# Latents and keys and values of both token halves made in tile pairs, in an attention stage between two expert layers

## The chip, the cores and the metric

One Trainium2 chip, one of its cores. The metric is device time in microseconds of one execution, the median of the timed runs. Engines are called as the profile calls them: PE (TensorE's matmuls), PEld (its weight loads), DVE (VectorE), ACT (ScalarE), POOL (GpSimd), SP (SyncE, which here only issues DMAs).

## What is computed

A macaron block: half of a mixture of experts on the layer-normalized tokens, attention, half of the same mixture again, each added to its input. 16 batches of 1024 tokens, 256 wide; 8 experts, the best 2 of each token. The attention, which the change touches:

```python
q = x @ W_q                                   # x: normalized, 16 x 1024 x 256
latent_kv = (x @ W_k + x @ W_v) @ W_down_kv   # 64 wide
k_rec = latent_kv @ W_up_k                    # 16 heads of 16
v_rec = latent_kv @ W_up_v
scores = (q k_rec^T) / sqrt(256) * exp(-0.01 |t - t'|)
out = softmax(scores) v_rec
return out @ W_o
```

All matmuls touched by the change are in fp32, which PE runs as two passes each.

## The kernel before

Three stages follow each other: the first mixture, the attention (class `Attention`), the second mixture. The attention runs all engines over one list, `self.plan`, that `order()` writes out in advance. Every engine walks through the whole list and executes its own part of each item, with waits on semaphores between engines; so the list sets the order on each engine's queue, POOL's and SP's too.

**The loop of the plan.** Heads go in pairs, 8 pairs a batch, 128 pairs in all. `order()` loops over `s`; one pass is called a slot here. Its main item is `("step", score, turn)`: four score pieces (L1163; q times k for 512 keys each, into the ring of four banks 0 to 3, read by DVE's row maxima at L1453 or, once in eight slots, by a multiply at L1448) and four turned pieces (L1172 and L1176; scores transposed, into the ring of three banks 5 to 7, read by ACT's exponential at L1376). The score pieces run 12 slots ahead of the turned ones. At the end of a slot stands `("W", p, kb)` (L1312): four matmuls of 17 columns in four column tiles, that weigh the values. Between step and W a slot takes what is due: every eighth slot the maxima of a pair (`max`, L1457 and L1462) and, in that slot and the next, a `sub` on POOL each (L1691), then norm, output projection (`out`, L1288), routing of the tokens for the next stage (`r_...` items, with POOL's centers at L1672, and its scatters, four indirect DMAs at L1684), and one portion each of two generators: `gather_order(b + 1)` (tokens of the next batch: gathers, two indirect DMAs each at L1613, adds at L1620 and L1622, centers, transposes "turn") and `unit_order(b)`. `None` in a generator ends its portion, so it says how many slots the generator takes.

**`unit_order(b)`**, for b of 1 to 15: two slots of latents (one chunk of 512 tokens each), 8 projections of six slots each, four slots of values. Projections 0 to 3 are queries (two halves of the heads times two chunks), 4 to 7 keys. A projection is made by PE in a bank of the score ring (L1220 queries, L1223 keys), read by DVE twice with the decay factors (L1551, into buffer `qs[:, i % 2]`), and split into three bf16 parts: `cast` 0 (ACT, L1349), `rest` 0 (POOL, L1651), two slots on `cast` 1, one slot later `rest` 1, one slot later the next projection. `send` writes the parts to HBM, `stack` fetches them in the layout of a head pair. At L1551's item DVE waits for `part_lo` of projection i - 2, that is for its second `rest`, since that is when its `qs` buffer is free. The gathers of the next batch begin in the slot after projection 3. Batch 0 has no steps beside it and another order; its rests are made by DVE.

**Latents, keys, values.** A latent (L1208) takes a turn bank, and PE multiplies 128 rows by 64 columns, twice 128 rows deep; ACT copies 64 x 512 to `lat` (L1343). A key projection is one matmul 64 rows deep, over the chunk's 512 columns of `lat`. A values unit is two matmuls 64 rows deep (L1230), and ACT copies it to `V` (L1354).

Of the kernel before, what the change touches and what calls it, by code (L numbers as in the profile page):

```python
# [700 lines left out]
class Attention:  # L701
# [4 lines left out]
    def __init__(self, nc, sig, x0, ys, tables, x1, x2, parts, mdram, xs, routes, cst, w, begin):  # L706
# [12 lines left out]
        self.XR, self.xT, self.lat = sb("XR", [128, 8, D]), sb("xT", [128, 2, S]), sb("lat", [DL, S])  # L719
# [9 lines left out]
        self.wd, self.wuk, self.wuv = sb("wd", [128, 2, DL]), sb("wuk", [DL, D]), sb("wuv", [DL, D])  # L729
# [27 lines left out]
        self.loaded, self.x_in = sig.new("a_loaded", 16 * 15), sig.new("a_x_in", 48 * B)  # L757
# [139 lines left out]
    def unit_order(self, b):  # L897
        for ch in range(2):
            yield from (("latent", b, ch), None)
        if not b:  # L900
            for i in range(0, 8, 2):
# [4 lines left out]
                if i == 2:  # L906
                    yield from (("values", 0, t2) for t2 in range(4))
            return
        for i in range(8):
            yield from (("project", b, i), None, ("cast", b, i, 0), None, ("rest", b, i, 0))  # L910
            if i:
                yield ("send", b, i - 1)
            yield from (None, None, ("cast", b, i, 1), None, ("rest", b, i, 1), None)
        for t2 in range(4):
            yield ("values", b, t2)
            if t2 == 2:
# [141 lines left out]
    def sync(self, e, w):  # L1058
# [8 lines left out]
        for dst, src in ((self.ident[:], cst["ident"]), (self.decay[:, 0], cst["decn"]), (self.decay[:, 1], cst["decp"]),  # L1067
                         (self.Dm[:], cst["dm"]), (self.wq[:], fold(wt["q"])), (self.wk[:], fold(wt["k"])),
                         (self.wv, fold(wt["v"])), (self.wd[:], fold(wt["down"])), (self.wuk[:], wt["upk"]),
                         (self.wuv[:], wt["upv"]), (self.wo[:], fold(wt["o"])),  # L1070
# [79 lines left out]
    def tensor(self, e, w, ps, bank):  # L1150
# [3 lines left out]
        w.wait_ge(*self.loaded.at(240))  # L1154
# [24 lines left out]
        for item in self.plan:  # L1179
# [23 lines left out]
            if kind == "latent":  # L1203
                b, ch = at
                w.wait_ge(*self.result("weight", 2))
                w.wait_ge(*self.result("turn", b, ch, 1))
                for k in range(2):
                    ins = e.matmul(to[0:DL, 0:512], self.wkv[:, k, :], self.xT[:, k, 512 * ch:512 * ch + 512], start=(k == 0), stop=(k == 1))  # L1208
                ins.then_inc(self.filled.sem, 1)
            if kind == "project":  # L1210
# [3 lines left out]
                w.wait_ge(*self.s_read.at(z - 3))  # L1214
                of = bank[z % 4]
                z += 1
                if not keys:
                    w.wait_ge(*self.result("turn", b, ch, 1))
                    for k in range(2):
                        ins = e.matmul(of, self.wq[:, k, 128 * hf:128 * hf + 128], self.xT[:, k, sl], start=(k == 0), stop=(k == 1))  # L1220
                else:
                    w.wait_ge(*self.result("latent", b, ch))
                    ins = e.matmul(of, self.wuk[:, 128 * hf:128 * hf + 128], self.lat[:, sl], start=True, stop=True)  # L1223
                ins.then_inc(self.s_filled.sem, 1)
            if kind == "values":
                b, t2 = at
                w.wait_ge(*self.result("latent", b, t2 // 2))
                for j in range(2):
                    t = 2 * t2 + j
# [568 lines left out]
```

## Time and profile before

| | |
|---|---|
| timed runs, us | 5887.23, 5893.35, 5893.88; median 5893.35 |
| span of the profiled execution, us | 6207.9 |
| the profiled execution's own time | not given |
| PE, DVE, ACT, POOL busy, share of the span | 88%, 74%, 53%, 45% |
| mean granted TensorE clock | 0.953 |

The span is from the first to the last instruction of one profiled execution, and it is 5.3% above the median of the timed runs. A row of a timeline gives the start, the busy time of the merged instructions and the idle time before them with what ended it. A matmul's duration includes its way through the array, so that successive ones overlap in the records.

### The profile page before, as it was taken

What the parts mean: (1) busy time and instruction counts of PE and PEld (TensorE: products, weight loads), DVE (VectorE), ACT (ScalarE), POOL (GpSimd) and SP (SyncE); (2) the same over time, 40 slices, a digit from 0 to 9 for tenths busy, and PEclk for the clock granted to TensorE, in tenths of its full rate; (3) what the DMA queues carried; (4) which work ended last, traced back from release to release, by engine and by line L of the source; (5) the groups of instructions that cost most, each with busy time, mean ns of one, the idle gap of its engine ahead of it and who ended that gap; (6) DMA issues with size and microseconds to landing.
All of it is one profiled execution on the core that took longest, in us unless ns stands there. A gap on an engine that the chain in (4) does not pass through costs nothing.

```text
span 6207.9 us, 114160 instructions
## 1 busy us (share of the span) xinstructions
PE 5474.1 (88%) x35792; PEld 3260.2 (53%) x35792; DVE 4582.3 (74%) x14351; ACT 3294.6 (53%) x6557; POOL 2823.2 (45%) x2857
## 2 busy tenths in 40 slices
PE   4459999389999999999999999999999996988874
PEld 4448888134444444444444444444444444877763
DVE  6545555577888888888888888888888994545554
ACT  1124444156666666666666666666666664433321
POOL 5650000263656656647557566476574333012244
PEclk9999999689999999999999999999999997999987
DMA  4433333444545554545545555454454443335555
GB/s 152 147 109 105 105 105 102 130 100 89 122 104 113 127 102 117 117 101 121 117 106 123 110 114 123 100 122 113 104 122 96 97 75 121 105 112 160 157 180 171
DMA packets 535036, 728.64 MB, mean 117 GB/s; under 512 B 79892, under 2 KB 450740, under 8 KB 534452
## 3 DMA queue, kind: packets, MB, share of 16 engines
q1 hardware_dynamic: 485300, 587.06, 39.3%
q0 software_dynamic: 49152, 134.28, 7.3%
q8 instruction: 307, 5.03, 0.4%
q14 instruction: 277, 2.27, 0.1%
HBM read 425.64 MB, written 295.44 MB: 116 GB/s over the span
## 4 chain that ended last, share of the span: by engine, by line
PE 76%; DVE 10%; another core or an unknown queue 4%; issue 4%; POOL 3%; ACT 2%; DMA 1%; SPq 1%; DVEq 0%; ACTq 0%; POOLq 0%
PE psum L1312 15%; PE psum L1163 14%; PE psum L395 12%; PE psum L1172 11%; PE psum L412 6%; PE psum L1176 3%; PE psum L403 2%; DVE at_mx L1453 2%; PE psum L384 2%; PE psum L1288 2%; PE psum L1220 2%; ACT at_P L1376 1%; PE psum L1208 1%; PE psum L1230 1%
## 5 line engine op out<-in xcount | busy, mean ns | idle before, releaser
L1376 ACT ACTIVATE at_P<-psum 128x512 f32<-128x512 f32 x4096 | 2131.2, 602 | 1098.5 <-PE psum L1172 577.0
L1453 DVE TENSOR_REDUCE at_mx<-psum 128x4 f32<-128x512 f32 x3584 | 2220.2, 681 | 286.9 <-PE psum L1163 260.5
L1163 PE MATMUL psum<-at_kst,at_qst 96*128 96x128 bf16 (+3 forms) x7168 | 1599.1, 293 | 55.0 <-DVE at_mx L1453 28.8
L1172 PE MATMUL psum<-at_qst,at_kst 99*128 99x512 bf16 (+3 forms) x5120 | 1465.4, 319 | 100.8 <-ACT at_P L1376 96.1
L1163 PEld LDWEIGHTS psum<-at_kst,at_qst 96*128 96x128 bf16 x7168 | 616.3, 99 | 1326.5 <-DVE at_mx L1453 520.7
L1312 PE MATMUL psum<-at_P,at_V 128*17 128x512 f32 x8192 | 1095.2, 607 | 0.0
L1691 POOL TENSOR_TENSOR at_Sd<-at_Sd,at_m 128x1024 f32<-128x1024 f32 x256 | 484.4, 1898 | 886.8 <-DVE at_m L1462 885.9
L1172 PEld LDWEIGHTS psum<-at_qst,at_kst 99*128 99x128 bf16 x5120 | 490.5, 98 | 251.1 <-ACT at_P L1376 129.9
L1176 PE MATMUL psum<-at_ident,at_Sd 128*128 128x128 f32 x2048 | 565.1, 276 | 0.0
L696 POOL DMA_INDIRECT m2Y<-ys,m2yi x256 | 243.9, 953 | 692.2 <-DMA ys<-m2X 370.7
L1448 DVE CUSTOM_DVE_ANT_0 at_Sd<-psum,at_Dm 128x128 f32<-128x128 f32 x2048 | 444.9, 286 | 148.3 <-PE psum L1163 86.5
L395 PE MATMUL psum<-m2wgu,m2xgT 128*128 x1680 | 464.1, 413 | 24.2 <-issue 14.3
L395 PE MATMUL psum<-m1wgu,m1xgT 128*128 x1584 | 412.4, 396 | 0.4 <-issue 0.3
L1651 POOL TENSOR_TENSOR at_qs<-at_qs,at_pt 128x1024 f32<-128x1024 f32 x120 | 256.2, 2135 | 248.9 <-ACT at_pt L1349 247.3
L395 PEld LDWEIGHTS psum<-m2wgu,m2xgT 128*128 128x128 f32 x1680 | 311.4, 198 | 89.5 <-issue 35.7
L610 DVE TENSOR_TENSOR m2X<-m2X,psum 128x256 f32<-128x256 f32 x280 | 117.5, 420 | 317.8 <-ACT m2X L445 229.5
L1651 POOL TENSOR_TENSOR at_pt<-at_qs,at_pt 128x1024 bf16<-128x1024 f32 x120 | 256.0, 2134 | 164.9 <-ACT at_pt L1349 163.2
L657 POOL DMA_INDIRECT xs<-m1X,m1idx x256 | 249.3, 974 | 164.0 <-DVE m1idx L499 90.8
L1176 PEld LDWEIGHTS psum<-at_ident,at_Sd 128*128 128x128 f32 x2048 | 290.2, 142 | 55.3
L1349 ACT ACTIVATE at_pt<-at_qs 128x1024 bf16<-128x1024 f32 x256 | 273.5, 1069 | 76.5 <-DMA parts<-at_pt 43.5
L1312 PEld LDWEIGHTS psum<-at_P,at_V 128*17 128x17 f32 x8192 | 136.8, 95 | 324.8 <-issue 316.5
L412 PE MATMUL psum<-m2wdn,m2hT 128*128 x1680 | 280.9, 305 | 29.8 <-DVE m2hT L619 16.1
(267 smaller groups left out, 7893.0 us busy)
## 6 DMA issues: line engine op xcount, KB each, us to landing
parts<-at_pt SPq DMA_DIRECT2D x768, 128.0 KB
at_qst<-parts SPq DMA_DIRECT2D x768, 128.0 KB
at_kst<-parts SPq DMA_DIRECT2D x128, 384.0 KB
m2X<-xs SPq DMA_DIRECT2D x280, 128.0 KB
ys<-m2X SPq DMA_DIRECT2D x280, 128.0 KB
m1X<-xs SPq DMA_DIRECT2D x264, 128.0 KB
ys<-m1X SPq DMA_DIRECT2D x264, 128.0 KB
at_kst<-parts SPq DMA_DIRECT2D x128, 256.0 KB
```

Source lines behind the costliest of these rows:

```text
L395: ins = e.matmul(gu, self.xgT[:, j % 3, p, 128 * (k // 3):128 * (k // 3) + 128], self.wgu[q][:, k // 3, bass.ds(expert[j] * 512, 512)], st ...
L412: ins = e.matmul(bank[6 + i % 2][:, 0:D], self.hT[:, i % 2, p, 128 * (k // 3):128 * (k // 3) + 128], self.wdn[q][:, k // 3, bass.ds(expert ...
L1163: ins = e.matmul(bank[z % 4][:, col - 512 * u:col - 512 * u + ln], self.qst[0:96, s, side, 128 * t:128 * t + 128], self.kst[0:96, s, 1 - s ...
L1172: ins = e.matmul(turns[a % 3][:, q0 - 512 * qh:q0 - 512 * qh + ln], self.kst[0:99, s, side, 128 * kb:128 * kb + 128], self.qst[0:99, s, 1 ...
L1176: ins = e.transpose(turns[a % 3][:, 128 * (kb % 4):128 * (kb % 4) + 128], self.Sd[:, (2 * p + hh) % 4, kb, :], self.ident[:])
L1312: ins = e.matmul(V[c:c + 17, :], self.V[:, b % 2, kb, 2 * (p % 8) + hh, :], self.P[:, self.p_slot(p, kb, hh) % NP, 512 * qh:512 * qh + 512 ...
L1349: e.activation(self.pt[:, j % 2, c], self.qs[:, i % 2], ACT.Copy).then_inc(self.part_hi.sem, 1)
L1376: e.activation(self.P[:, i % NP, 512 * qh:512 * qh + 512], turns[a % 3], ACT.Exp).then_inc(self.taken.sem, 1)
L1448: ins = e.tensor_tensor_reduce(self.Sd[:, (2 * p + hh) % 4, 4 * u + t, :], of[:, t], self.Dm[:], 1.0, LOWEST, ALU.mult, ALU.max, accum_out ...
L1453: e.tensor_reduce(self.mx[:, p % 2, hh, 8 * o + 4 * u:8 * o + 4 * u + 4], of, op=ALU.max, axis=AX.X).then_inc(self.s_read.sem, 1)
L1651: e.tensor_tensor(pt[:, j % 2, 2] if c else self.qs[:, i % 2], self.qs[:, i % 2], pt[:, j % 2, c], ALU.subtract).then_inc(self.part_lo.sem, 1)
L1691: e.tensor_tensor(sd, sd, self.m[:, p % 2, 8 * hh:8 * hh + 8].rearrange("p (t o) -> p t o", o=1).to_broadcast([128, 8, 128]), ALU.subtract ...
```

## The change

Latents of a batch are one item. PE writes chunk 0 to rows 0 to 63 and chunk 1 to rows 64 to 127 of one bank (two column tiles, in turn for each half of the depth), and ACT copies 128 x 512 at once. `lat` holds the two chunks on two halves of the partitions, and `wuk` and `wuv` are loaded twice, one copy for each half. Key projections 4 and 5, and 6 and 7, stand together in one slot: PE makes both, each from its half of the partitions (two row tiles) into a bank of its own, after waiting for both banks. Casts, rests and sends keep their distances. Values units 0 and 2, and 1 and 3, are made in pairs in the same manner, in two slots instead of four. In all, `unit_order` takes 51 slots instead of 54, and each projection stands one slot earlier.

```diff
-        self.XR, self.xT, self.lat = sb("XR", [128, 8, D]), sb("xT", [128, 2, S]), sb("lat", [DL, S])
+        self.XR, self.xT, self.lat = sb("XR", [128, 8, D]), sb("xT", [128, 2, S]), sb("lat", [128, 512])
...
-        self.wd, self.wuk, self.wuv = sb("wd", [128, 2, DL]), sb("wuk", [DL, D]), sb("wuv", [DL, D])
+        self.wd, self.wuk, self.wuv = sb("wd", [128, 2, DL]), sb("wuk", [128, D]), sb("wuv", [128, D])
...
-        self.loaded, self.x_in = sig.new("a_loaded", 16 * 15), sig.new("a_x_in", 48 * B)
+        self.loaded, self.x_in = sig.new("a_loaded", 16 * 17), sig.new("a_x_in", 48 * B)
...
-        for ch in range(2):
-            yield from (("latent", b, ch), None)
+        yield from (("latent", b), None)
...
-                    yield from (("values", 0, t2) for t2 in range(4))
+                    yield from (("values", 0, t2) for t2 in (0, 2, 1, 3))
...
-            yield from (("project", b, i), None, ("cast", b, i, 0), None, ("rest", b, i, 0))
+            if i < 4 or i % 2 == 0:
+                yield ("project", b, i)
+            if i >= 4 and i % 2 == 0:
+                yield ("project", b, i + 1)
+            yield from (None, ("cast", b, i, 0), None, ("rest", b, i, 0))
...
-        for t2 in range(4):
-            yield ("values", b, t2)
-            if t2 == 2:
+        for t2 in range(2):
+            yield from (("values", b, t2), ("values", b, 2 + t2))
+            if t2 == 1:
                 yield ("send", b, 7)
             yield None
...
-                         (self.wv, fold(wt["v"])), (self.wd[:], fold(wt["down"])), (self.wuk[:], wt["upk"]),
-                         (self.wuv[:], wt["upv"]), (self.wo[:], fold(wt["o"])),
+                         (self.wv, fold(wt["v"])), (self.wd[:], fold(wt["down"])), (self.wuk[0:DL], wt["upk"]), (self.wuk[DL:128], wt["upk"]),
+                         (self.wuv[0:DL], wt["upv"]), (self.wuv[DL:128], wt["upv"]), (self.wo[:], fold(wt["o"])),
...
             if kind == "latent":
-                b, ch = at
+                b = at[0]
                 w.wait_ge(*self.result("weight", 2))
-                w.wait_ge(*self.result("turn", b, ch, 1))
+                w.wait_ge(*self.result("turn", b, 1, 1))
                 for k in range(2):
-                    ins = e.matmul(to[0:DL, 0:512], self.wkv[:, k, :], self.xT[:, k, 512 * ch:512 * ch + 512], start=(k == 0), stop=(k == 1))
+                    for ch in range(2):
+                        ins = e.matmul(to[DL * ch:DL * ch + DL, :], self.wkv[:, k, :], self.xT[:, k, 512 * ch:512 * ch + 512], start=(k == 0), stop=(k == 1))
...
-                else:
-                    w.wait_ge(*self.result("latent", b, ch))
-                    ins = e.matmul(of, self.wuk[:, 128 * hf:128 * hf + 128], self.lat[:, sl], start=True, stop=True)
-                ins.then_inc(self.s_filled.sem, 1)
+                    ins.then_inc(self.s_filled.sem, 1)
+                elif ch == 0:
+                    w.wait_ge(*self.result("latent", b))
+                    w.wait_ge(*self.s_read.at(z - 3))
+                    for half, to in ((0, of), (1, bank[z % 4])):
+                        e.matmul(to, self.wuk[DL * half:DL * half + DL, 128 * hf:128 * hf + 128], self.lat[DL * half:DL * half + DL, :],
+                                 start=True, stop=True).then_inc(self.s_filled.sem, 1)
             if kind == "values":
                 b, t2 = at
-                w.wait_ge(*self.result("latent", b, t2 // 2))
-                for j in range(2):
-                    t = 2 * t2 + j
-                    ins = e.matmul(to[:, 256 * j:256 * j + 256], self.lat[:, 128 * t:128 * t + 128], self.wuv[:], start=True, stop=True)
-                ins.then_inc(self.filled.sem, 1)
+                if t2 < 2:
+                    w.wait_ge(*self.result("latent", b))
+                    w.wait_ge(*self.taken.at(a - 1))
+                    for j in range(2):
+                        t = 2 * t2 + j
+                        for half, to in ((0, turns[a % 3]), (1, turns[(a + 1) % 3])):
+                            ins = e.matmul(to[:, 256 * j:256 * j + 256], self.lat[DL * half:DL * half + DL, 128 * t:128 * t + 128],
+                                           self.wuv[DL * half:DL * half + DL, :], start=True, stop=True)
+                            if j == 1:
+                                ins.then_inc(self.filled.sem, 1)
...
             if kind == "latent":
-                b, ch = at
+                b = at[0]
                 if b:
                     w.wait_ge(*self.full("values", b - 1, 3))
-                e.activation(self.lat[:, 512 * ch:512 * ch + 512], of[0:DL, 0:512], ACT.Copy).then_inc(self.taken.sem, 1)
+                e.activation(self.lat[:], of, ACT.Copy).then_inc(self.taken.sem, 1)
```

## Rows read from the trace of the kernel before

**Rows 1.** The page's head and its busy times.

```profile
span 6207.9 us, 114160 instructions
...
PE 5474.1 (88%) x35792; PEld 3260.2 (53%) x35792; DVE 4582.3 (74%) x14351; ACT 3294.6 (53%) x6557; POOL 2823.2 (45%) x2857
```

**Rows 2.** Busy time by stretch, then granted clock, DMA share, GB/s: one batch, two short stretches.

```profile
2720.70:2965.50 244.80, 236.04 (x1630) 114.50 (x1628) 209.28 (x654) 162.12 (x299) 147.66 (x146) 0.98 0.52 114
2853.44:2860.27 6.83, 4.77 (x15) 3.97 (x15) 4.16 (x33) 3.12 (x5) 5.77 (x6) 0.50 1.03 190
2880.75:2884.16 3.41, 3.41 (x16) 1.79 (x14) 2.98 (x9) 1.79 (x3) 3.16 (x5) 0.50 0.93 280
```

**Rows 3.** Timeline of PE: start, busy, instruction; a latent and the W behind it.

```profile
2720.78 1.93 PE L1208 MATMUL psum<-at_xT,at_wkv 128*64 128x512 f32 x4
2722.64 1.05 PE L1312 MATMUL psum<-at_P,at_V 128*17 128x512 f32 x8
```

**Rows 4.** Timeline of PE: a key projection and a values unit, each with its W.

```profile
2622.18 1.12 PE L1223 MATMUL psum<-at_lat,at_wuk 64*128 64x512 f32 x2
2623.24 1.05 PE L1312 MATMUL psum<-at_P,at_V 128*17 128x512 f32 x8
...
2669.68 1.13 PE L1230 MATMUL psum<-at_wuv,at_lat 64*128 64x256 f32 x4
2670.74 1.05 PE L1312 MATMUL psum<-at_P,at_V 128*17 128x512 f32 x8
```

**Rows 5.** Groups of instructions between 2600 and 3080 us: ACT's exponentials.

```profile
L1376 ACT ACTIVATE at_P<-psum 128x512 f32<-128x512 f32 x500 | 260.4, 602 | 131.9 <-PE psum L1172 70.5 <-PE psum L1176 47.9 <-remote 10.9
```

**Rows 6.** The same groups on POOL: busy us, mean ns, idle before.

```profile
L1691 POOL TENSOR_TENSOR at_Sd<-at_Sd,at_m 128x1024 f32<-128x1024 f32 x30 | 56.8, 1898 | 95.5 <-DVE at_m L1462 95.4
...
L1684 POOL DMA_INDIRECT xs<-at_RX,at_idx x32 | 32.0, 999 | 9.7 <-issue 7.4 <-POOL at_idx L1681 2.3
L1613 POOL DMA_INDIRECT at_xT<-ys,at_yib x30 | 29.2, 974 | 8.8 <-issue 7.6 <-PE psum L1172 1.2
...
L1622 POOL TENSOR_TENSOR at_XR<-at_XR,at_xT 128x1024 f32<-128x1024 f32 x8 | 18.9, 2358 | 0.6
L1672 POOL TENSOR_SCALAR at_RX<-at_ob,at_rmv,at_rrs 128x256 f32<-128x256 f32 x14 | 17.1, 1222 | 0.1
L1620 POOL TENSOR_TENSOR at_xT<-at_xT,at_gab 128x1024 f32<-128x1024 f32 x8 | 15.2, 1897 | 5.1 <-DMA at_xT<-ys,at_yib 5.0
```

**Rows 7.** Timeline of POOL in batch 7; in brackets the idle time before and what ended it.

```profile
2807.14 1.90 POOL L1691 TENSOR_TENSOR at_Sd<-at_Sd,at_m 128x1024 f32<-128x1024 f32 x1 [1.78 <-DVE at_m L1462]
...
2816.05 0.97 POOL L1613 DMA_INDIRECT at_xT<-ys,at_yib  x1 [0.16 <-issue]
...
2818.31 2.13 POOL L1651 TENSOR_TENSOR at_pt<-at_qs,at_pt 128x1024 bf16<-128x1024 f32 x1
...
2835.68 1.90 POOL L1691 TENSOR_TENSOR at_Sd<-at_Sd,at_m 128x1024 f32<-128x1024 f32 x1 [0.39 <-DVE at_m L1462]
```

**Rows 8.** Timeline of DVE in the same batch.

```profile
2810.52 4.85 DVE L1453 TENSOR_REDUCE at_mx<-psum 128x4 f32<-128x512 f32 x8
...
2817.54 1.29 DVE L1551 TENSOR_TENSOR at_qs<-psum,at_decay 128x512 f32<-128x512 f32 x2 [0.65 <-PE psum L1223]
```

**Rows 9.** Timeline of PE in the same batch: starts of score pieces, two waits.

```profile
2809.19 0.39 PE L1163 MATMUL psum<-at_kst,at_qst 96*128 96x512 bf16 x1
...
2812.23 0.39 PE L1163 MATMUL psum<-at_kst,at_qst 96*128 96x512 bf16 x1
...
2813.62 0.38 PE L1163 MATMUL psum<-at_kst,at_qst 96*128 96x128 bf16 x2
...
2855.50 0.61 PE L1172 MATMUL psum<-at_qst,at_kst 99*128 99x512 bf16 x1 [3.88 <-ACT at_P L1376]
...
2866.05 0.38 PE L1163 MATMUL psum<-at_kst,at_qst 96*128 96x512 bf16 x1
...
2879.51 0.17 PE L1260 MATMUL psum<-at_O,at_tri 128*128 128x8 bf16 x1 [2.39 <-DVE at_mx L1453]
```

More of the change, by code:

```diff
@@ L1153, in tensor @@
         fence(w, self.begin)
-        w.wait_ge(*self.loaded.at(240))
+        w.wait_ge(*self.loaded.at(272))
         w.wait_ge(*self.w_ready.at(2))
@@ L1213, in tensor @@
                 sl = slice(512 * ch, 512 * ch + 512)
-                w.wait_ge(*self.s_read.at(z - 3))
                 of = bank[z % 4]
@@ L1217, in tensor @@
                 if not keys:
+                    w.wait_ge(*self.s_read.at(z - 4))
                     w.wait_ge(*self.result("turn", b, ch, 1))
@@ L1336, in scalar @@
                     w.wait_ge(*self.turned_read(b - 1))
-                    w.wait_ge(*self.full("latent", b - 1, 1))
+                    w.wait_ge(*self.full("latent", b - 1))
                 e.activation(self.xT[:, k, 512 * ch:512 * ch + 512], of, ACT.Copy).then_inc(self.taken.sem, 1)
             if kind == "latent":
-                b, ch = at
+                b = at[0]
                 if b:
                     w.wait_ge(*self.full("values", b - 1, 3))
-                e.activation(self.lat[:, 512 * ch:512 * ch + 512], of[0:DL, 0:512], ACT.Copy).then_inc(self.taken.sem, 1)
+                e.activation(self.lat[:], of, ACT.Copy).then_inc(self.taken.sem, 1)
             if kind == "cast":
@@ L1389, in vector @@
         e.memset(bank[4], 0.0).then_inc(self.v_zero.sem, 1)
-        w.wait_ge(*self.loaded.at(240))
+        w.wait_ge(*self.loaded.at(272))
         first, fin, base, NR = self.routes.first, self.routes.fin, self.base, self.routes.NR
@@ L1583, in pick @@
         u, tt = 4 * b + t2, slice(8 * b + 2 * t2, 8 * b + 2 * t2 + 2)
-        w.wait_ge(*self.loaded.at(240))
+        w.wait_ge(*self.loaded.at(272))
         w.wait_ge(*self.r_logits.at(u + 1))
@@ L1610, in gpsimd @@
                     w.wait_ge(*self.turned_read(b - 1))
-                    w.wait_ge(*self.full("latent", b - 1, 1))
+                    w.wait_ge(*self.full("latent", b - 1))
                 for k in range(2):
```

## The prediction

> **What bounds the kernel now.** The profiled execution's span is 6207.9 us [rows 1]; the three timed runs have a median of 5893.35 us, which the span exceeds by 5.3%, and no time of its own is given for the profiled execution. So sums made on rows are differences, which I put on the median, and I say below which row I trust least for that reason. I read the page first, then the stretch table, then TensorE's timeline. The page shows PE busy 88% of the span [rows 1]. The stretch of one whole batch of the attention (244.8 us from one batch's latents to the next) has PE busy 236.04, DVE 209.28, ACT 162.12, POOL 147.66 [rows 2]. TensorE is what ends last; of its 8.8 idle us two waits explain 6.3 (3.88 and 2.39 us [rows 9]). Only a microsecond of TensorE is worth a microsecond here.
>
> I call a slot one pass of the plan's loop: a step (4 score pieces, 4 turned pieces), whatever else is due, and one W. A bare slot is 3.0 us on PE (2809.19 to 2812.23 [rows 9]). In it DVE reads four banks, 2.4 us (eight took 4.85 [rows 8]), and ACT four, at 602 ns each [rows 5]. So DVE has about half a microsecond of slack in a bare slot, and the ring of four score banks lets TensorE run at most four pieces ahead of it.
>
> **What is removed, batch by batch.** Latents: four matmuls of one chunk are four passes, and PE spends 1.86 us from their start to the start of the W that follows [rows 3]. Afterwards both chunks run in two column tiles. That column tiles overlap is shown by W itself: eight passes of 512 columns in 1.05 us, where the four latent passes take 1.93 [rows 3]. So the second chunk is free: 1.86 us less. Keys: one projection costs 1.06 us up to W [rows 4]; four become two pairs, 2.12 us less. Values: one unit costs 1.06 us up to W [rows 4]; four become two pairs, 2.12 us less. Row tiles, which the last two rest on, appear nowhere in this trace; their bounds are full overlap (2.12 and 2.12) and none (0 and 0). I take full overlap, since the nearest row, W with four tiles, is a full one. The Trainium skill (TensorE: Matmul & The Clock Gate, Part 3: Packing small matmuls) says that tiles in different row groups run concurrently and gives 3.07x for four; no row here shows it. One evacuation of latents by ACT also goes, 0.6 us of an engine with a third of its time free: nothing.
>
> **What is added.** A values pair waits for two of the three turn banks, so for one more exponential than before; one takes 0.6 us [rows 5]. Bounds for two pairs are 0 (ACT already done) and 1.2 us a batch; I take 1.0, since in these slots ACT is the last to finish. Two more weight loads of 64 KB (17 instead of 15) are issued at the start of the stage, where tokens and gathers still come in: 0, and at most some 1.3 us of issuing if that cover were gone. The gain side is 1.86 + 2.12 + 2.12 - 1.0 = 5.1 us a batch.
>
> **The pair of keys 4 and 5.** Both projections now come to DVE in the same slot. DVE writes the second into the buffer that projection 3 used, and waits at L1551 for the second "rest" of projection 3, a POOL subtraction. In the plan that rest stands one slot ahead of projection 4, and projection 5 used to stand six slots later. Before, in batch 7, the rest of projection 3 ran on POOL 2818.31 to 2820.44 [rows 7], while projection 4 was read 2817.54 to 2818.83 [rows 8]: the wait that never mattered would already be 1.6 us.
>
> It gets longer, since units now start one slot earlier against the rest of the plan (one latent slot, not two). I go by batch 7. POOL is released by the row maxima at 2807.14 [rows 7]; behind that stand, in its queue, two subs, a routing center, gathers and then the rest. In the new order one gather fewer stands between (the one of 2816.05 to 2818.31 moves ahead), and rest 3 ends 2.26 us earlier, at 2818.2. But projection 4 is a whole slot earlier: it stands behind the score pieces that DVE reads from 2810.52 [rows 8]; they end at 2812.95, and projection 4 at 2814.3. Projection 5 then waits until 2818.2 and ends at 2819.5. Behind it on DVE stand the score reads of the next slot, and TensorE's fourth score piece of that slot needs projection 5's bank. That piece started at 2813.62 [rows 9]; with the pair ahead of it 2814.7 would be its time, and it starts at 2819.5: **TensorE is held 4.8 us**, the wait for two free banks included. A hold of 2.39 us [rows 9] was followed by 3.41 us at a granted clock of 0.50, that is 1.2 of 2.4 GHz [rows 2], and the same work takes half as long at 1.00: 1.7 us more. The 3.88 us hold [rows 9] was followed by 6.83 us at 0.50, 4.77 of them busy [rows 2]: 2.4 us. I take the smaller. Together 6.5 us.
>
> The Trainium skill (TensorEngine Tiling (Array Packing), PSUM Bottleneck) warns that tiling speeds TensorE but not the evacuation of PSUM. By that alone the pair would cost its two reads on DVE (2.6 us [rows 8]) against slack of the ring, some 0.5 us of hold a pair, and the batch would still win; this sentence and the last are not in the sum.
>
> **The pair of keys 6 and 7.** Projection 7 waits likewise for the second rest of projection 5. From the release of POOL by the maxima in the slot of 2835.68 [rows 7] that queue then holds two subs (1.90 each), a center (2 x 1.22), three gathers (two DMAs each, 0.97 and 0.30 between), a routing scatter (four DMAs at 1.00 and 0.30 between), one add (1.90 and 2.36) [rows 6], and two rests (2.13 [rows 7]): 3.8 + 2.4 + 7.6 + 5.2 + 4.3 + 4.3 = 27.6 us, and 1.3 for projection 7, 28.9. On TensorE the stretch from the same release to the piece that needs the bank (2866.05 [rows 9]) was 30.4 us; less one single key and with a pair and its two banks it is 31.0. So no hold: 0. But those 30.4 us hold the 3.88 us standstill and its 2.4 us of slow clock [rows 9, 2]. It stands where SP and POOL issue DMAs together (its gap ends at 2855.50, between the slots of 2835.68 and 2866.05, where the queue above has its gathers), and the profile is 5.3% longer than the timed runs. If it isn't in a timed run, TensorE needs 24.7 us against 28.9: 4.2 held and 1.7 of clock, 5.9. I take the middle, 3.0.
>
> **Sum.** A steady batch changes by -5.1 + 6.5 + 3.0 = +4.4 us; 13 of them (2 to 14): +57. Batch 15 has no gathers behind it: rest 3 ends 8.4 us after the release at 2807.14, at 2815.5, projection 5 at 2816.8, a hold of 2.1 against a gain of 5.1: -3. Batch 1 fills an uneven stage: 0. Batch 0: the latents must wait for all turns, -1. 5893.35 + 53 = **5946 us**.
>
> **Rivals.** (a) *POOL is in time, the tiles pay.* TensorE's share speaks for it, and that rest 3 was only 1.6 us behind. With the wait as it lay before, the hold is some 2.1 us at the first pair and 0.9 at the second, too short for the clock: -5.1 + 3.0 = -2.1 in 15 batches, **5861 us**; with no hold at all, 5817. It decides below 5.1 us of holds a batch. Against it: the projections move a slot earlier against the subs. (b) *Only the first pair holds*, and the standstill at 2851.6 goes since the gathers move: +1.4 or, without the clock, -0.3 a batch: **about 5900 us**. (c) *Row tiles don't overlap*: keys and values gain nothing, 4.2 us a batch more: 4.4 + 4.2, 13 times: **about 6001 us**. Against it stands W.
>
> **Chances.** Forecast 0.52, (a) 0.24, (b) 0.17, (c) 0.07. A change within 0.2% (12 us) can't be told from none. The forecast and (c) are slower, (a) is faster, (b) is split 0.02 faster, 0.10 same, 0.05 slower: faster 0.26, same 0.10, slower 0.64. The forecast's own range runs from +1.4 (no second hold) to +7.3 a batch (a full one): 5908 to 5984. The range for all of it, 5850 to 6005, reaches over (b) and the milder half of (a) and leaves out the case without any hold and the worse half of (c).
>
> **What would show it.** On TensorE: key and value matmuls start in pairs some ns apart, and the latents' eight passes take 1.9 us; if they stand in file, (c). On DVE: the second key projection starts just after a POOL L1651 ends, with an idle time of over 3 us put down to it. On TensorE the fourth score piece after the pair of 4 and 5 starts some 5 us late in batches 2 to 14, and the granted clock falls to 0.50 behind it. PE's busy time in a batch falls, while the batch grows from 244.8. I am wrong if the batch is shorter, and wrong in the reason if it is longer without those waits.

## The result, and the profile after

| | before | after |
|---|---|---|
| timed runs, median (lowest to highest), us | 5892.54 (5887.23 to 5893.88), 4 runs | 5945.31 (5940.97 to 5953.12), 4 runs |
| ratio, 95% interval | | 1.0093 [1.0081, 1.0105] |
| span of the profiled execution, us | 6207.9 | 5945.6 (its own time 5947.44) |

The change makes the kernel 52.8 us slower, where 53 was forecast. The sign, the place of the loss and its trigger came out as written. That the sum fits to a microsecond is luck in part: errors in its terms cancel (see Sum below).

The head and the busy times of the page of the kernel after; they answer to [rows 1].

```profile
span 5945.6 us, 114177 instructions
...
PE 5337.0 (90%) x35792; PEld 3213.9 (54%) x35792; DVE 4574.3 (77%) x14351; ACT 3284.0 (55%) x6541; POOL 2828.8 (48%) x2857
...
PE 67%; POOL 16%; DVE 8%; issue 4%; ACT 1%; DMA 1%; SPq 1%; POOLq 0%; DVEq 0%; ACTq 0%
```

PE's busy time fell by 137 us, and the last line, the chain that ended last, gives POOL 16% of the span (3% in the profile of before). The two profiles don't compare, though: that of before is 5.3% above its timed runs, that of after is not. Of the 13 points of POOL most are not the change's: e11 below, a kernel without any tile pair, has 12% there in a profile that is as short as its timed runs. The experiments below had to settle why.

The timeline of TensorE after, in batch 7: start, busy, instruction, idle before and what ended it. The rows answer to [rows 3, 4, 9].

```profile
2640.54 1.94 PE L1212 MATMUL psum<-at_xT,at_wkv 128*64 128x512 f32 x8
2642.41 1.05 PE L1324 MATMUL psum<-at_P,at_V 128*17 128x512 f32 x8
...
2728.41 1.13 PE L1230 MATMUL psum<-at_lat,at_wuk 64*128 64x512 f32 x4 [0.47 <-DVE at_mx L1465]
2729.47 1.05 PE L1324 MATMUL psum<-at_P,at_V 128*17 128x512 f32 x8
...
2736.45 0.61 PE L1166 MATMUL psum<-at_kst,at_qst 96*128 96x128 bf16 x2 [4.44 <-DVE at_qs L1563]
...
2777.47 0.39 PE L1175 MATMUL psum<-at_qst,at_kst 99*128 99x512 bf16 x1 [2.81 <-ACT at_P L1388]
...
2789.19 0.39 PE L1166 MATMUL psum<-at_kst,at_qst 96*128 96x512 bf16 x1 [2.26 <-DVE at_qs L1563]
...
2802.95 0.17 PE L1272 MATMUL psum<-at_O,at_tri 128*128 128x8 bf16 x1 [2.06 <-DVE at_mx L1465]
...
2832.80 1.14 PE L1240 MATMUL psum<-at_wuv,at_lat 64*128 64x256 f32 x8 [0.38 <-ACT at_P L1388]
2833.86 1.05 PE L1324 MATMUL psum<-at_P,at_V 128*17 128x512 f32 x8
```

The tiles overlap: eight latent passes take 1.94 us where four took 1.93, and a pair of keys (four passes) reaches the W behind it in 1.06 us, as one projection did before. The new idle time stands where score pieces wait for DVE's read of a projection (4.44 and 2.26 us), and once where turned pieces wait for an exponential (2.81).

The timelines of DVE and POOL around the pair of keys 4 and 5, after. First DVE, then POOL.

```profile
2729.57 1.29 DVE L1563 TENSOR_TENSOR at_qs<-psum,at_decay 128x512 f32<-128x512 f32 x2
2735.10 1.29 DVE L1563 TENSOR_TENSOR at_qs<-psum,at_decay 128x512 f32<-128x512 f32 x2 [4.24 <-POOL at_pt L1663]
```

```profile
2724.21 1.91 POOL L1703 TENSOR_TENSOR at_Sd<-at_Sd,at_m 128x1024 f32<-128x1024 f32 x1
2726.10 2.44 POOL L1684 TENSOR_SCALAR at_RX<-at_ob,at_rmv,at_rrs 128x256 f32<-128x256 f32 x2
2728.70 1.04 POOL L1625 DMA_INDIRECT at_xT<-ys,at_yib  x1 [0.16 <-issue]
2730.04 0.96 POOL L1625 DMA_INDIRECT at_xT<-ys,at_yib  x1 [0.30 <-issue]
2731.02 1.91 POOL L1703 TENSOR_TENSOR at_Sd<-at_Sd,at_m 128x1024 f32<-128x1024 f32 x1
2732.87 2.13 POOL L1663 TENSOR_TENSOR at_pt<-at_qs,at_pt 128x1024 bf16<-128x1024 f32 x1
```

DVE reads projection 4, then stands 4.24 us for the second rest of projection 3, which POOL reaches only after two subs, a center and a gather. Rest 3 ends at 2735.00, projection 5 is read at 2735.10, and the score piece that needs its bank starts when that read is over.

Two stretches of the kernel after, with the granted clock as the third number from the end: the batch, then the time behind that hold. They answer to [rows 2].

```profile
2640.50:2884.30 243.80, 230.87 (x1631) 112.76 (x1630) 209.26 (x654) 160.66 (x298) 147.69 (x146) 0.97 0.52 114
...
2735.01:2741.84 6.83, 5.39 (x21) 4.01 (x25) 4.37 (x7) 0.60 (x1) 4.18 (x2) 0.50 0.00 0
```

PE is busy 230.87 us in a batch instead of 236.04. But the batch is not longer than in the profile of before: 243.8 against 244.8 us. The prediction had said "I am wrong if the batch is shorter". The row of before was not taken at the speed of its timed runs, as the experiments show, so this test can't be read from the two rows.

### The profile page after: what moved, and what is told of

The parts are those of the page before. It is cut to its first block, busy times and chain, and to the rows that moved or that the text cites. A ratio compares the mean times of both kernels' runs of the same rounds, so it can differ in the third digit from the quotient of the medians.

```text
span 5945.6 us, 114177 instructions
## 1 busy us (share of the span) xinstructions
PE 5337.0 (90%) x35792; PEld 3213.9 (54%) x35792; DVE 4574.3 (77%) x14351; ACT 3284.0 (55%) x6541; POOL 2828.8 (48%) x2857
## 3 DMA queue, kind: packets, MB, share of 16 engines
q14 instruction: 276, 2.26, 0.1%
## 4 chain that ended last, share of the span: by engine, by line
PE 67%; POOL 16%; DVE 8%; issue 4%; ACT 1%; DMA 1%; SPq 1%; POOLq 0%; DVEq 0%; ACTq 0%
PE psum L395 13%; PE psum L1324 13%; PE psum L1166 12%; PE psum L1175 9%; PE psum L412 7%; POOL xs L657 4%; POOL at_xT L1625 3%; DVE at_mx L1465 3%; PE psum L1179 3%; PE psum L1300 2%; POOL at_Sd L1703 2%; PE psum L384 2%; PE psum L403 2%; PE psum L1224 2%; DVE at_Sd L1460 2%
## 5 line engine op out<-in xcount | busy, mean ns | idle before, releaser
L1166 PE MATMUL psum<-at_kst,at_qst 96*128 96x128 bf16 (+3 forms) x7168 | 1603.1, 294 | 128.9 <-DVE at_qs L1563 79.2
L1324 PE MATMUL psum<-at_P,at_V 128*17 128x512 f32 x8192 | 1108.3, 613 | 0.0
L395 PE MATMUL psum<-m2wgu,m2xgT 128*128 x1680 | 442.5, 399 | 6.2 <-issue 4.8
L1361 ACT ACTIVATE at_pt<-at_qs 128x1024 bf16<-128x1024 f32 x256 | 273.9, 1071 | 119.2 <-POOL at_qs L1663 52.7
L1625 POOL DMA_INDIRECT at_xT<-ys,at_yib x248 | 245.2, 989 | 190.9 <-PE psum L1224 119.4
L395 PEld LDWEIGHTS psum<-m2wgu,m2xgT 128*128 128x128 f32 x1680 | 298.6, 190 | 63.9 <-issue 13.8
L610 DVE TENSOR_TENSOR m1X<-m1X,psum 128x256 f32<-128x256 f32 x264 | 111.1, 421 | 263.9 <-ACT m1X L445 263.9
L395 PEld LDWEIGHTS psum<-m1wgu,m1xgT 128*128 128x128 f32 x1584 | 280.3, 189 | 47.6 <-issue 1.2
```

Of the source, the lines that this page charges most:

```text
L395: ins = e.matmul(gu, self.xgT[:, j % 3, p, 128 * (k // 3):128 * (k // 3) + 128], self.wgu[q][:, k // 3, bass.ds(expert[j] * 512, 512)], st ...
L1166: ins = e.matmul(bank[z % 4][:, col - 512 * u:col - 512 * u + ln], self.qst[0:96, s, side, 128 * t:128 * t + 128], self.kst[0:96, s, 1 - s ...
L1324: ins = e.matmul(V[c:c + 17, :], self.V[:, b % 2, kb, 2 * (p % 8) + hh, :], self.P[:, self.p_slot(p, kb, hh) % NP, 512 * qh:512 * qh + 512 ...
L1625: e.indirect_dma_start(rows[:, 2 * t + k, :], None, self.ys, bass.IndirectOffsetOnAxis(ap=self.yib[:, 4 * half + t, k:k + 1], axis=0)).the ...
```

## The experiments

The experiments ran on four chips, called A to D here, and chips differ in speed. On A, B and C the kernel before took 6236.98, 6239.70 and 6236.67 us; on D it took 5888.26, about as in the timing of the result. The first profile of before, with its span of 6207.9 us, is of the slower sort by its length. So times are compared with before on the same chip. "Period" below is the mean distance between the latents of batches 3 to 14, in the one execution that was profiled. e0, e1, e2 and e3 ran on A, e4, e6, e7 and e8 on B, e9 and e10 on C, e11 and e12 on D.

| kernel | us | before on the same chip | ratio, 95% interval | period, us |
|---|---|---|---|---|
| e0 before | 6241.16 | 6236.98 | 1.0004 [0.9993, 1.0014] | 245.83 |
| e2 latents tiled, keys and values single | 6142.37 | 6236.98 | 0.9845 [0.9829, 0.9862] | 239.48 |
| e1 e2 with values in pairs | 6127.17 | 6236.98 | 0.9819 [0.9803, 0.9836] | 238.13 |
| e3 after with four qs buffers | 6135.49 | 6236.98 | 0.9826 [0.9810, 0.9843] | 238.93 |
| e6 after | 6223.76 | 6239.70 | 0.9976 [0.9967, 0.9986] | 245.15 |
| e8 before | 6238.25 | 6239.70 | 0.9999 [0.9986, 1.0013] | 245.82 |
| e4 after, latents take two slots | 6217.33 | 6239.70 | 0.9965 [0.9954, 0.9976] | 245.21 |
| e7 e3 and e4 together | 6166.52 | 6239.70 | 0.9881 [0.9853, 0.9910] | 240.89 |
| e9 e3, casts of projection 5 later | 6112.29 | 6236.67 | 0.9797 [0.9777, 0.9818] | 237.22 |
| e10 before | 6235.70 | 6236.67 | 0.9999 [0.9988, 1.0009] | 246.11 |
| e11 before, both latents in one slot | 5906.19 | 5888.26 | 1.0031 [1.0020, 1.0043] | 239.69 |
| e12 after, keys 6 and 7 single | 5939.73 | 5888.26 | 1.0085 [1.0068, 1.0102] | 242.96 |
| the after of the result | 5945.31 | 5892.54 | 1.0093 [1.0081, 1.0105] | 243.88 |

### e0, e8, e10: the kernel before again

No edit. They ask whether the standstill of 3.88 us [rows 9] belongs to one execution. None of the three ran on a chip of 5893 us, so how before looks there stays unseen.

> The kernel before, unchanged, profiled once more. If the 3.88 us standstill of TensorE near 2851 us and the slow clock behind it belong to that one profiled execution, this profile has a span near 5892 us and the standstill is gone or much shorter in every batch. If they belong to the kernel, they are there again in each of batches 2 to 14 and the second pair's hold had to be small.

> The kernel before, unchanged, for a profile from the same chip as the changed kernel's. On a chip of 5893 us: no standstill of about 4 us near the slot of the second half's gathers, a batch of about 240 us. On a chip of 6237 us: the standstill as before.

> The kernel before once more, for its profile, should this call's chip be of the quick kind (5893 us): then a batch takes 240 to 241 us and there is no standstill of 4 to 5 us at the second half's gathers. On a chip of 6237 us: 245.8 us a batch, with it.

Timelines of e0 in batch 8: TensorE, DVE, ACT.

```profile
3116.18 0.61 PE L1172 MATMUL psum<-at_qst,at_kst 99*128 99x512 bf16 x1 [4.93 <-ACT at_P L1376]
```

```profile
3115.43 0.29 DVE L1448 CUSTOM_DVE_ANT_0 at_Sd<-psum,at_Dm 128x128 f32<-128x128 f32 x1 [6.06 <-remote]
```

```profile
3115.53 2.06 ACT L1376 ACTIVATE at_P<-psum 128x512 f32<-128x512 f32 x4 [6.30 <-remote]
```

Three engines stand at once. TensorE names ACT, ACT and DVE name nothing that the profile knows ("remote"). Meanwhile POOL issues six gathers in a row and SP fifteen DMAs in 8 us:

```profile
3106.31 0.97 POOL L1613 DMA_INDIRECT at_xT<-ys,at_yib  x1 [0.16 <-issue]
...
3112.58 0.94 POOL L1613 DMA_INDIRECT at_xT<-ys,at_yib  x1 [0.30 <-issue]
```

```profile
3104.33 3.65 SPq L1096 DMA_DIRECT2D parts<-at_pt  x6
3108.52 2.74 SPq L1109 DMA_DIRECT2D at_qst<-parts  x6
3111.30 1.37 SPq L1111 DMA_DIRECT2D at_kst<-parts  x3
```

The standstill is there in all three traces: TensorE stands for 2.6 to 5.2 us at this place in every batch from 2 to 13, but for one batch of e10. So it belongs to the kernel on these chips and not to one execution. Each of the three is on a chip where before takes over 6235 us. What in the two bursts delays the others was not taken apart.

### e2 and e1: latents alone, then latents and values

```diff
# e2, against after: keys and values one at a time again, each from its half
-            if i < 4 or i % 2 == 0:
-                yield ("project", b, i)
-            if i >= 4 and i % 2 == 0:
-                yield ("project", b, i + 1)
-            yield from (None, ("cast", b, i, 0), None, ("rest", b, i, 0))
+            yield from (("project", b, i), None, ("cast", b, i, 0), None, ("rest", b, i, 0))
...
-        for t2 in range(2):
-            yield from (("values", b, t2), ("values", b, 2 + t2))
-            if t2 == 1:
+        for t2 in range(4):
+            yield ("values", b, t2)
+            if t2 == 2:
# e1: the first of these two edits alone
```

> Latents by two column tiles in one slot; keys and values one at a time, from their half of the partitions. Theory (TensorE ends last, what costs is the wait of a paired key projection for POOL's rest): 1.86 us a batch less, about 5863 us. Rival (moving all projections one slot earlier against subs and routing is what costs): no gain or a loss, 5892 us or more.

> Latents in column tiles and values in pairs of row tiles, keys one at a time. Theory: 1.86 + 2.12 - 1.0 = 3.0 us a batch less, about 5845 us. Rival (a values pair's wait for two turn banks eats what it saves): like the latents alone, about 5863 us.

e2 gains 94.6 us, or 6.35 a batch by the period, far more than the 1.86 that was expected and that the tiles explain. The rest goes with the standstill, which is gone from e2's trace from batch 2 on. Units start a slot earlier there, and the two bursts lie otherwise. POOL and SP in e2, batch 8:

```profile
3044.46 0.96 POOL L1617 DMA_INDIRECT at_xT<-ys,at_yib  x1 [0.16 <-issue]
...
3048.23 0.94 POOL L1617 DMA_INDIRECT at_xT<-ys,at_yib  x1 [0.30 <-issue]
```

```profile
3050.50 2.66 SPq L1108 DMA_DIRECT2D at_qst<-parts  x6
```

The gathers in a row are four instead of six, and they end before SP's fetches begin, where in e0 the fetches ran in the middle of them. That this is what frees the other engines fits, and was not isolated (e4 and e7 below, where the slot is put back, bear on it). e1 is 15.2 us faster than e2, 1.0 a batch. That is 0.24%, and the two intervals still touch; the periods, 1.35 us apart, point the same way. The prediction had 2.12 - 1.0 = 1.1.

### e6, e3, e4, e7: the after, its qs buffers, and the shift back

```diff
# e3, against after, five places of this kind
-        self.qs = sb("qs", [128, 2, 2, 512])
+        self.qs = sb("qs", [128, 4, 2, 512])
...
-                w.wait_ge(*self.part_lo.at(4 * (i // 2) if not b else max(16, 2 * (8 * b + i - 1))))
+                w.wait_ge(*self.part_lo.at(4 * (i // 2) if not b else max(16, 2 * (8 * b + i - 3))))
# e4, against after
-        yield from (("latent", b), None)
+        yield from (("latent", b), None, *((None,) if b else ()))
```

> The changed kernel, unchanged, against the kernel before on the chip of this call. Chips differ: one runs the kernel before in 5893 us, another in 6237 us, and there TensorE stands still for 4 to 5 us once in each batch, which the sum counted at half. If that standstill is in the kernel before alone, then on a chip of 6237 us the change costs about 0 (ratio 0.995 to 1.003), and on a chip of 5893 us it costs 0.9% again.

> The whole change, but with four buffers qs instead of two, so that projection i waits for the rest of i - 4 and not of i - 2. Theory: both holds go (4.45 us before the fourth score piece, some 2.3 at the second pair, and a slow clock behind them), 8 to 9 us in 13 batches: 5820 to 5840 us, and no wait of L1563 for POOL in the profile. Rival (two evacuations of key banks in one slot are what DVE can't take): the holds stay within a microsecond of what they are, 5930 us or more.

> The whole change, but the latents take two slots of the plan again (one of them empty), so that projections stand where they stood against subs, gathers and routing. Theory (the shift by one slot lengthened the hold at the pair 4 and 5 from 2.1 to 4.8 us): about 2 to 3 us a batch less than the changed kernel and less slow clock, 0.5 to 1% faster than it. Rival (the shift does nothing, the wait is POOL's speed alone): within 0.2% of the changed kernel.

> Four buffers qs and latents in two slots. With four buffers alone there remained one hold of 2.8 us a batch: ACT's cast of projection 5 waits for a rest that POOL does late, and exponentials stand behind it. Theory: that wait hangs on the shift by a slot too and goes, 3 to 4 us a batch less than with four buffers alone. Rival: it stays, and the time is that of four buffers alone (0.983 of the kernel before on a chip of 6237 us).

e6 is as expected, by its ratio no slower than before on this chip. e6 minus e1 is what the pairs of keys do, on two chips with nearly equal times of before: +96.6 us, 7.0 a batch by the period. Two more buffers take back 88.3 us, 6.2 a batch (e3), where 8 to 9 were expected. The groups of DVE's reads of projections from 1300 to 5000 us, in e6 and then in e3: busy, mean ns, idle before and what ended it.

```profile
L1563 DVE TENSOR_TENSOR at_qs<-psum,at_decay 128x512 f32<-128x512 f32 x240 | 154.3, 686 | 120.4 <-POOL at_pt L1663 72.6 <-PE psum L1224 39.0 <-PE psum L1230 7.8
```

```profile
L1563 DVE TENSOR_TENSOR at_qs<-psum,at_decay 128x512 f32<-128x512 f32 x240 | 151.8, 685 | 48.6 <-PE psum L1224 38.9 <-PE psum L1230 9.2
```

The 72.6 us behind POOL vanish, and what the other two releasers cost hardly moves. 72.6 over 15 batches is 4.8 us; the period falls by 6.2, and the time at a granted clock of 0.50 from 14.6 to 9.3 us a batch. This is the run that shows the cause; the theory holds in its mechanism, and the 2.8 us hold by ACT stays. e3, with everything the change does, is still no faster than e1, which makes keys one at a time.

e4 puts the slot back that the latents lost. The wait on POOL falls to 42.3 us, and the kernel gains 0.1%, inside the intervals. The groups of score pieces, turned pieces and routing in e4 and then in e6, same stretch:

```profile
L1166 PE MATMUL psum<-at_kst,at_qst 96*128 96x128 bf16 (+3 forms) x6782 | 1511.9, 293 | 54.9 <-DVE at_qs L1563 47.4 <-DVE at_mx L1465 4.7 <-DMA at_kst<-parts 1.0
L1175 PE MATMUL psum<-at_qst,at_kst 99*128 99x512 bf16 (+3 forms) x4847 | 1394.5, 320 | 81.0 <-ACT at_P L1388 70.0 <-issue 10.9
...
L1263 PE MATMUL psum<-at_rw,at_rxT 128*128 128x8 f32 x456 | 60.1, 258 | 14.9 <-DVE at_mab L1460 11.2 <-DVE at_mx L1465 2.6 <-issue 0.9
```

```profile
L1166 PE MATMUL psum<-at_kst,at_qst 96*128 96x128 bf16 (+3 forms) x6781 | 1505.6, 292 | 80.1 <-DVE at_qs L1563 75.8 <-DMA at_kst<-parts 3.7
L1175 PE MATMUL psum<-at_qst,at_kst 99*128 99x512 bf16 (+3 forms) x4845 | 1388.7, 319 | 73.0 <-ACT at_P L1388 40.9 <-issue 31.4
...
L1263 PE MATMUL psum<-at_rw,at_rxT 128*128 128x8 f32 x456 | 58.9, 256 | 1.7 <-DVE at_mx L1465 0.2
```

The hold of scores is 25 us less in the 15 batches, but turned pieces wait 8 more, and the routing 13 more. The rival's number came true (within 0.2%), but not its reason: the wait on POOL does hang on the slot (72.6 against 42.3), as the prediction said with "gets longer". With four buffers the added slot costs time: e7 is slower than e3, 0.9881 against 0.9826 and 2.0 us a batch, which neither of its two expectations had.

Part of what eats the gain shows in the same traces. With the slot back, POOL's six gathers in a row are back, and so are waits that name nobody. DVE in e4, batch 8:

```profile
3094.40 0.29 DVE L1460 CUSTOM_DVE_ANT_0 at_Sd<-psum,at_Dm 128x128 f32<-128x128 f32 x1 [4.88 <-remote]
```

Over batches 1 to 14 DVE's idle time without a known releaser ("remote") is 79.2 us in e0, 48.2 in e4 and 21.1 in e7, against 1.5 in e6, 5.5 in e3 and 3.8 in e2. So the slot decides on these chips whether the standstill is there, and e4 and e7 are no clean test of what the slot does to the hold at the keys: they take the one away and bring part of the other back.

### e9: what is left of the second hold

```diff
# against e3
-            yield from (None, None, ("cast", b, i, 1), None, ("rest", b, i, 1), None)
+            if i == 5:
+                yield from (None, None, None, ("cast", b, i, 1), None, ("rest", b, i, 1))
+            else:
+                yield from (None, None, ("cast", b, i, 1), None, ("rest", b, i, 1), None)
```

> Four buffers qs, latents in one slot, and the second cast and rest of projection 5 one slot later. Theory (the hold of 2.8 us left with four buffers is ACT, that waits in this cast for POOL's first rest of projection 5, with the exponentials of the next step behind it): it goes, with its slow clock 3 to 4.5 us a batch, 0.8 to 1.1% of the time below the kernel with four buffers alone, so about 0.973 of the kernel before on a chip of 6237 us, the fastest of all. Rival (TensorE runs into the next thing that POOL is late with): less than half of that, 0.979 or more.

The 2.81 us hold of the kernel after has another trigger than the first. POOL, then ACT in the after:

```profile
2773.70 2.14 POOL L1663 TENSOR_TENSOR at_qs<-at_qs,at_pt 128x1024 f32<-128x1024 f32 x1
```

```profile
2775.87 1.06 ACT L1361 ACTIVATE at_pt<-at_qs 128x1024 bf16<-128x1024 f32 x1 [3.24 <-POOL at_qs L1663]
2776.83 2.04 ACT L1388 ACTIVATE at_P<-psum 128x512 f32<-128x512 f32 x4
```

ACT's second cast of projection 5 waits 3.24 us for its first rest, with the exponentials behind it in ACT's queue, and TensorE waits for those. e3 still has this hold (2.82 us). In e9 it is split into holds of 1.20 and 1.53, ACT's idle time before L1361 and its like falls from 72.3 to 35.9 us, and the period by 1.7, where 3 to 4.5 were expected. By the ratios, 0.9797 against e3's 0.9826, this is the rival's case (0.979 or more). e9 is the fastest of its sort of chip. It was not timed on D, nor on the chip of the result, so that it beats the kernel before there too is not shown.

### e11 and e12: the shift alone, the first pair alone

```diff
# e11, against before
-        for ch in range(2):
-            yield from (("latent", b, ch), None)
+        yield from (("latent", b, 0), ("latent", b, 1), None)
# e12, against after
-            if i < 4 or i % 2 == 0:
+            if i != 5:
                 yield ("project", b, i)
-            if i >= 4 and i % 2 == 0:
+            if i == 4:
                 yield ("project", b, i + 1)
```

> The kernel before, with nothing changed but the plan: both latents of a batch, each made as before, stand in one slot, so that every later unit moves one slot earlier. On a chip of 6237 us the latents alone gave 6.35 us a batch, where the column tiles should give 1.86. Theory: the other 4.5 us are the standstill, and it is the shift by a slot that ends it, so this kernel has it no more and takes about 0.989 of the kernel before (241.3 us a batch). Rival (the column tiles gave it all, by freeing ACT and TensorE): 0.998 to 1.002, with the standstill.

> The whole change, but keys 6 and 7 one at a time, in the slots they had before; keys 4 and 5 stay a pair. Theory (each pair has its own hold by POOL's rest, the first 4 to 4.5 us and the second 2 to 2.5, with a slow clock behind): 2 to 3.5 us a batch less than the changed kernel, on a chip of 6237 us 0.989 to 0.993 of the kernel before. Rival (what is gained at one pair is lost again further on, since POOL is as late as before): within 0.2% of the changed kernel, 0.996 to 1.000.

On D before takes 5888.26 us, and the shift, which on the others goes with the loss of the standstill, costs 0.31%. So the theory could not be put to the test here as worded: there seems to be no standstill to lose. By period, e11 has 239.69 us. Its timed median is 17.9 us above that of before, 1.2 for each of 15 batches; its profiled execution, the fastest of its seven (5897.23), is 9.0 above, 0.6 each. That would put before at some 238.5 to 239.1 here, about 7 less than on the other chips. It is an estimate: no profile of before was taken on such a chip, and what the shift costs there was not traced to a wait. e11's TensorE has, per batch, a hold of 1.75 us behind DVE's maxima, with a granted clock of 0.50 for 3.41 us, and one of 1.58 us before turned pieces:

```profile
2729.84 0.49 PE L1162 MATMUL psum<-at_kst,at_qst 96*128 96x256 bf16 x2 [1.75 <-DVE at_mx L1452]
2755.80 0.39 PE L1171 MATMUL psum<-at_qst,at_kst 99*128 99x512 bf16 x1 [1.58 <-ACT at_P L1375]
```

```profile
2730.01:2733.42 3.41, 3.41 (x15) 1.96 (x14) 3.41 (x7) 1.79 (x3) 2.73 (x12) 0.50 0.64 127
```

The hold of 1.58 us is a short form of the after's 2.81: ACT's cast waits for the same rest on POOL, with no pair in the kernel.

```profile
2754.20 1.06 ACT L1348 ACTIVATE at_pt<-at_qs 128x1024 bf16<-128x1024 f32 x1 [2.01 <-POOL at_qs L1650]
```

So this hold is not the pair's alone; in the after it is longer.

The rival to e11's theory, that the column tiles ended the standstill, is answered on the slower chips: e4 and e7 keep the tiles, and with the slot put back the waits that name nobody return.

e12 takes the second pair away. Its first hold is 4.44 us still, and that of 2.26 us is gone:

```profile
2733.33 0.61 PE L1166 MATMUL psum<-at_kst,at_qst 96*128 96x128 bf16 x2 [4.44 <-DVE at_qs L1567]
2774.70 0.61 PE L1175 MATMUL psum<-at_qst,at_kst 99*128 99x512 bf16 x1 [2.80 <-ACT at_P L1392]
```

But two single projections cost 1.06 us more on TensorE than a pair, and 1.0085 is not told apart from the 1.0093 of the change, timed on another chip. By the period e12 is 0.9 us a batch below the change, where 2 to 3.5 were expected. The rival was right: the second pair gives back about what its tiles gain. The loss against e11 on the same chip, 33.5 us, sits at the first pair, with keys 4 and 5, as the forecast had it.

## Why the prediction was right, and where it was not

**The bound.** TensorE ends last: right. Its waits and its slow clock account for the growth of the batch to within 0.6 us (Sum below), and in e3 the batch shrinks when they go.

**What is removed.** Latents 1.86: right by the passes (1.94 us for both chunks), not measured as time by itself, since the shift goes with it. Keys and values, 1.06 us for each single one: right by the rows; the bound "no overlap" and with it rival (c) fall. The Trainium skill (TensorE: Matmul & The Clock Gate, Part 3: Packing small matmuls), which has row tiles run concurrently, agrees with the trace here: four passes in the time of two. e1 against e2 makes the values 15.2 us faster, 1.0 a batch, where 1.1 was forecast, the bank wait included (a values pair waits 0.38 us for ACT, 0.8 a batch against the 1.0 taken).

**The pair of keys 4 and 5.** Forecast: a hold of 4.8 us, the wait for two banks in it, and 1.7 for the clock. Measured: 0.47 and 4.44, together 4.91, caused by the second rest of projection 3 on POOL. DVE's wait was forecast as 2818.2 - 2814.3 = 3.9 us and is 4.24. The clock's share was too small: 6.83 us at 0.50, of them 5.39 busy, which is 2.7 lost instead of 1.7. I took the smaller of two rows, and [rows 2] had the larger one, 2.4, beside it.

**The pair of keys 6 and 7.** Forecast: the middle (3.0) of no hold, if the standstill is in a timed run, and 5.9, if it is not. The reasons hold, but the middle was no case of its own: on a chip with before at 5888 us the second case seems to apply, and by the prediction's own working that was +7.3 us a batch and 5984 us. What was measured in the stretch is 2.26 held by projection 7 and 2.81 held by ACT's cast of projection 5. The latter I had not named: the prediction followed only the buffer's wait, DVE for the second rest, and not ACT's own wait for the first rest, though the cast stands in the same chain. The sum of the two, 5.07, lies above the 4.2 worked out. Both are followed by time at 0.50 in places:

```profile
2789.62:2793.03 3.41, 3.41 (x15) 1.11 (x15) 2.55 (x7) 1.54 (x2) 3.33 (x2) 0.50 0.53 173
```

**The shift of one slot.** The prediction gave it a part in rest 3's wait and no price of its own. e11 gives it one: +0.31% alone (17.9 us), where the total is 52.8. That term was missing. On the slower chips it has the other sign: the loss of the standstill gives about 4.5 us a batch back (e2, 6.35 less the 1.86 of the tiles), which no case of the prediction counted, not even (b), which names that loss.

**Sum.** Forecast +4.4 us a batch over 13 batches, 57. From e11 to the after, on chips with before at 5888 to 5893 us, the median grows by 39.1 us, the profiled executions differ by 50.2, and the period by 4.2, which is a figure of those executions. One batch checks it (243.80 us against 238.98 in e11, both batch 7). Gains: 1.7 (e11's two latents take 3.65 us, the after's 1.94), 2.1 and 2.1. Idle time above 0.8 us or caused by bank waits, after: 4.44, 0.47, 2.81, 2.26, 2.06, 0.38; e11: 1.75, 1.58, 0.95, 2.42; the difference is 5.7. Time at 0.50: 13.65 us after against 3.41, of it 12.21 against 3.41 busy, which is 4.4 lost. That makes 5.7 + 4.4 - 5.9 = +4.2 of 4.8; 0.6 stays unassigned. Nearly half of what the change puts on is the clock. The whole traces agree: 526 us at 0.50 in the after, 379 in e11. By the starts of the batches in the two traces, batches 2 to 14 take 53 us more in the after, batch 1 1.5 less, batch 15 with what follows it in the attention 2.5 less, what stands ahead of batch 1 1.2 less; the forecast had +57, 0, -3 and -1.

So +4.4 was met by terms that miss in both directions. The second pair's term was 2.1 us too small (3.0 against 5.07), the clock's 2.7 (1.7 against 4.4), and the wait of 2.06 us before the routing was in no term. Against that the sum took nothing off for the waits that a kernel without pairs has itself, 6.70 us in e11. In its reasons the forecast was right, in its closeness lucky.

**The rivals.** (a) needed POOL in time; it was not. It also held waits of 2.1 us to be too short for the clock; in the after holds of 2.26 and 2.06 us were each followed by 3.41 us at 0.50. With DVE's wait on POOL taken away, e3 gives 0.9826 on a chip where the lost standstill is in that number too, and it does not beat e1 (0.9819). So the gain that (a) had for pairs of keys did not come even then. ACT's hold of 2.8 us stands there, with more time at 0.50 than in e1 (9.3 us a batch against 4.0); e9, which splits it, has a period 0.9 us below e1's. (b), that only the first pair holds and the standstill goes, is the nearest by number for the other chips: there e6 is 0.9976, and (b) had 5900 over 5893.35, 1.0011. The standstill is gone there, but the second pair holds too, 2.0 us in batch 8. So the same change is slower on one sort of chip and slightly faster on the other. What differs most is the before: by the periods it has a standstill in a batch to lose on the one (245.8 us) and, by the estimate at e11, not on the other (238.5 to 239.1), while the period of the after differs by 1.3 us (245.15 and 243.88).

**The line I distrusted.** The prediction called the 5.3% between span and timed runs the reason to doubt the 3.88 us standstill. Right to doubt it: e0, e8 and e10 show it on chips of the slower sort, and nothing shows it on one of the result's speed. The standstill is not most of the difference between chips, however. Outside the attention the stages differ too: from the end of the last W on, e6 takes 1063.9 us against 883.7 in the after of the result. What makes these stages slower was not tried.

## What to carry to other kernels

Pairing matmuls in tiles pays on TensorE as the pass counts say, but it also brings their readers together: look up which buffer the second reader writes, who frees it, and where that release stands in its queue. A hold of two or three microseconds can cost more than its length: behind that of 4.44 us the clock was at 0.50 for 6.83 us, behind 2.26 and 2.06 for 3.41 each, though not behind e11's 2.42. So price a hold with its slow stretch, and buy a buffer before packing a producer. Where a profile's span is several per cent off the timed runs, forecast for each of the two kernels it could be, and don't take a middle.

## What the runs showed that was not expected

- One kernel takes 5888 to 5893 us on some chips and 6235 to 6241 on others, 5.9% apart. The mean granted clock of before is 0.968 to 0.970 on D and 0.949 to 0.954 on A to C. Taking only the two levels 1.00 and 0.50, that is some 365 against 599 us at 0.50; even if TensorE was busy all that time, the difference costs 117 of the 349 us, an estimate. The stretches ahead of the attention's first transposes and behind its last W take 1082.3 and 883.7 us in the after of the result, 1148.4 and 1063.9 in e6.
- By the same reckoning the kernel before on D has 365 us at 0.50 and the after of the result, at a mean of 0.956, 526 by its trace: up to 80 us lost by the clock, where the whole change costs 52.8. That is an estimate over two chips, and it doesn't say how much of the clock's fall the waits caused.
- On the slower chips DVE and ACT stand for some 6 us, with no releaser known, when POOL's run of six gathers meets SP's fifteen DMAs (6.06 and 6.30 us in e0). In e1, e2, e3 and e6, which move the units by one slot, this is gone from batch 2 on; in e4 and e7, which move them back, part of it returns. e9's DVE has none of it, but its ACT still has such waits of 3.4 to 4.1 us in most batches.
- A hold of 1.75 us was followed by 3.41 us at 0.50 in e11, less than the 2.39 us from which the prediction argued [rows 9], while the hold of 2.42 us in the same batch was followed by none. Holds of 1.20 and 1.53 us in e9, batch 8, were followed by none either. So in these traces the length of a hold alone doesn't tell whether the clock falls.
